# A transformer layer on one core: the first batch's cross tiles move from beside the end of the attention to the middle of it

## The reference

```python
x = x + attn(layernorm(x), wq, wk, wv, wo)      # 32 query heads, 8 key/value heads, head width 64, rope, causal
x = x + xattn(layernorm(x), ctx_2048)           # ctx: (4, 512, 512)
x = x + moe(layernorm(x), Wg, W1, W3, W2, sw1, sw3, sw2)
# xattn: both operands are rounded to fp8 (e4m3) steps in blocks, then out[e,m,n] = sum_k xq[e,m,k] * wq[e,n,k]
#   activations: blocks of 1 token x 128,  scale = max|x| of the block / 448
#   context:     blocks of 128 x 128,      scale = max|w| of the block / 448
# moe: top-1 of 8 experts, 256 places each, hidden width 704, silu(x@W1)*(x@W3) @ W2, plus one shared expert
```

## Time and profile before

| | |
|---|---|
| median of 3 runs | 1580.55 us (1579.67 to 1581.69) |
| the profiled execution's own time | 1581.1 us |
| its span | 1579.3 us |
| PE busy | 1453.4 us (92%) |
| DVE busy | 1205.1 us (76%) |
| POOL busy | 1022.9 us (65%) |
| ACT busy | 959.4 us (61%) |

### The profile page before, as it was taken

How to read it: one execution, slowest core, us unless ns; L and a number is a source line. 1 busy time by engine, 2 the same in 40 slices (tenths; PEclk the granted TensorE clock), 3 DMA queues, 4 the chain that set the end, 5 groups by cost and what they waited for, 6 DMA issues and landing times.

```text
span 1579.3 us, 26942 instructions
## 1 busy us (share of the span) xinstructions
PE 1453.4 (92%) x8617; PEld 1274.5 (81%) x8617; DVE 1205.1 (76%) x2936; ACT 959.4 (61%) x2420; POOL 1022.9 (65%) x1006
## 2 busy tenths in 40 slices
PE   5899999999999999999999997758988887999997
PEld 4788888888878888888888886648888787899996
DVE  7678888887887887887887887976676755577775
ACT  4687777777676787887887886432121213556562
POOL 3787887887777888888898896732121213345555
PEclk9999999999999999999999999888999999899998
DMA  6435534333322433433443432121000003577766
GB/s 205 139 101 165 158 103 128 116 85 109 115 60 59 107 105 90 115 98 95 115 111 86 113 94 67 54 83 60 27 28 28 8 28 124 179 228 223 228 214 237
DMA packets 106812, 177.08 MB, mean 112 GB/s; under 512 B 16886, under 2 KB 38646, under 8 KB 106672
## 3 DMA queue, kind: packets, MB, share of 16 engines
q1 hardware_dynamic: 103920, 166.84, 35.8%
q0 software_dynamic: 2560, 8.25, 1.6%
q10 hardware_dynamic: 192, 0.26, 0.1%
HBM read 97.31 MB, written 31.98 MB: 82 GB/s over the span
## 4 chain that ended last, share of the span: by engine, by line
PE 67%; DVE 15%; ACT 8%; issue 4%; DMA 3%; POOL 2%; SPq 1%; DVEq 0%; ACTq 0%; POOLq 0%
PE bank L429 15%; PE bank L431 14%; PE bank L430 14%; PE bank L481 6%; PE bank L447 4%; PE bank L496 4%; PE bank L497 4%; PE bank L448 4%; ACT P L811 3%; DVE P L1110 2%; PE bank L421 1%; ACT xnx L833 1%; DVE Opair L1145 1%; ACT Otmp L817 1%; DVE work L1059 1%
## 5 line engine op out<-in xcount | busy, mean ns | idle before, releaser
L811 ACT ACTIVATE P<-P,mn 128x512 f32<-128x512 f32 (+3 forms) x512 | 284.8, 557 | 210.5 <-DVE mn L1110 206.6
L1532 POOL TENSOR_TENSOR P<-P,ri 128x128 f32<-128x128 f32 (+3 forms) x512 | 361.4, 737 | 22.4 <-DVE ri L1099 22.3
L1110 DVE CUSTOM_DVE_ANT_0 P<-bank,mask 128x512 f32<-128x512 f32 (+3 forms) x512 | 236.6, 480 | 97.2 <-PE bank L448 95.6
L1151 DVE TENSOR_TENSOR PTl<-bank,PTh 128x512 fp32r<-128x512 f32 (+1 forms) x384 | 229.8, 599 | 33.5 <-ACT PTh L823 30.9
L481 PE MATMUL bank<-ident,P 128*128 128x128 f32 x1280 | 202.6, 273 | 2.5 <-POOL P L1532 2.5
L823 ACT ACTIVATE PTh<-bank 128x512 fp32r<-128x512 f32 (+1 forms) x384 | 197.9, 516 | 6.3 <-PE bank L481 3.2
L447 PE MATMUL bank<-KT,QT 128*128 128x256 f32 (+2 forms) x512 | 188.7, 369 | 10.9 <-DVE mn L1110 10.9
L496 PE MATMUL bank<-PTh,VS 128*128 128x256 f32 (+2 forms) x512 | 163.2, 329 | 13.0 <-DVE PTl L1151 8.9
L429 PE MATMUL bank<-XT,Wh 128*128 128x512 f32 x384 | 162.8, 424 | 9.3 <-DVE XT L1081 3.5
L448 PE MATMUL bank<-KT,QT 128*128 128x256 f32 (+2 forms) x512 | 166.3, 325 | 0.0
L497 PE MATMUL bank<-PTl,VS 128*128 128x256 f32 (+2 forms) x512 | 156.9, 327 | 0.0
(11 more groups left out here) (202 smaller groups left out, 4231.9 us busy)
## 6 DMA issues: line engine op xcount, KB each, us to landing
RW<-in_wf SPq DMA_DIRECT2D x170, 256.0 KB, 3.1
QT<-qh SPq DMA_DIRECT2D x256, 64.0 KB, 2.0
QT<-ql SPq DMA_DIRECT2D x252, 64.0 KB, 2.0
Oraw<-in_wo SPq DMA_DIRECT2D x16, 512.0 KB, 5.3
KT<-KT SPq DMA_DIRECT2D x32, 256.0 KB, 3.0
xnx<-in_ctx SPq DMA_DIRECT2D x32, 256.0 KB, 3.5
Wraw<-in_wqkv SPq DMA_DIRECT2D x9, 768.0 KB, 5.0
saved<-Wh SPq DMA_DIRECT2D x7, 768.0 KB, 3.5
```

Source lines behind the costliest of these rows:

```text
L811: e.activation(pq, pq, ACT.Exp, bias=mn[:, z, qb:qb + 1], scale=-1.0, accum_out=rs[:, z, qb:qb + 1]).then_inc(a_exp, 1)
L1110: e.tensor_tensor_reduce(P[:, z, off[qb]:off[qb] + k], bank[n % 2][:, 0:k], mask[:, 512 - k:512], -0.125, BIG, ALU.add, ALU.min, mn[:, z, ...
L1151: e.tensor_tensor(pt_part(PTl, part), bank[2 + part][:, 0:128 * n].rearrange("p (m n) -> p m n", n=128), pt_part(PTh, part).bitcast(F32), ...
L1532: e.tensor_tensor(pq, pq, ri[:, z, qb:qb + 1].to_broadcast([128, n]), ALU.mult).then_inc(g_norm, 1)
```

## The change

1. `cross_round` of batch 0 (4 tiles) leaves the side slots. Its tiles become four more jobs beside the attention; there are 20 jobs, one every 3 steps from 59 on, in four buffers instead of two. Their statistics are taken on ACT in steps 64 to 72, their inverse roots by DVE and POOL in steps 73 to 76, their block maxima in steps 77 to 82 (ACT norms a tile, DVE reduces it: `look`), and one call makes the scales of all four tiles in step 83 (`first_scales`). ACT norms the tile again when its job comes (`norm_beside`).
2. In a job the DVE parts come one step later than before; `unscaled` comes 6 steps behind `scaled`, so both fall in the same step, every third.
3. The Newton steps of the inverse roots in steps 18, 22 and 26 go to POOL (`newton`).
4. A step from 117 on runs two side slots instead of one, the second at its end. Batch 0's turns, products, norms and expert turns are spread over steps 121 to 130, the context turns of batch 1 go to steps 131 and 132. On DVE the first side slot of a step comes behind `masked(h, 1)` and `join` instead of in front.
5. The statistics behind a `cross_add` become a stage of their own, one slot later (`stats3`).
6. The first weight pieces are loaded in step 126 instead of 128; ACT and POOL split all 11 `Uh` pieces before they wait for the small tables, and the 6 `Dh` pieces inside the first parts of `ffn`.

```diff
@@ def slots():
     first = ("route_turn", "cross_turn", "logits", "choose", "place", "cross_product")
-    for b in range(NB):
+    for i in range(TB):
+        plan(-36 + i, "context_turn", 0, i)
+        plan(-32 + 2 * i, "cross_turn", 0, i)
+        plan(-31 + 2 * i, "cross_product", 0, i)
+        plan(-30 + 2 * i, "stats3", 0, i)
+        plan(-22 + i, "norm3", 0, i)
+        plan(-20 + i, "route_turn", 0, i)
+        plan(-16 + i, "context_turn", 1, i)
+    plan(-23, "rstd3", 0)
+    plan(-4, "logits", 0)
+    plan(-2, "choose", 0)
+    plan(2, "place", 0)
+    for b in range(1, NB):
         s = 16 * (b - 1)
...
@@ def background():
-    return [61 + 4 * j for j in range(NCTX)]
+    return [59 + 3 * j for j in range(NCTX + TB)]
...
+        jobs = [("context", t) for t in range(8)] + [("cross", t) for t in range(TB)]
+        jobs += [("context", t) for t in range(8, NCTX)]
+        YB = [xnx[:, 0, :], xnx[:, 1, :], free_wraw[:, 0:512], free_wraw[:, 512:1024]]
...
@@ scalar_engine
+            def norm_beside(j):
+                t = jobs[j][1]
+                wait_job_buffer(need, j)
+                need.wait_ge(g_root, 25)
+                e.activation(YB[j % 4], X[:, t, :], ACT.Identity, bias=ssum[:, 0, t:t + 1],
+                             scale=rstd[:, t:t + 1]).then_inc(a_norm, 1)
...
-                if h - 6 in begins:
-                    unscaled(begins[h - 6])
+                if h - 7 in begins:
+                    unscaled(begins[h - 7])
                 if h - 1 in begins:
                     scaled(begins[h - 1])
+                if h + 1 in begins and jobs[begins[h + 1]][0] == "cross":
+                    norm_beside(begins[h + 1])
+                if 77 <= h < 81:
+                    look(h - 77)
...
+            for s in (-8, -7, -6):
+                side_slot(s)
+            while len(pieces) > NP - UP:
+                split_piece(0, pieces.pop(0))
             need.wait_ge(d_k, 48)
...
@@ vector_engine
+            def first_scales():
+                need.wait_ge(v_look, TB)
+                scales(aam[:, :, :], asc[:, :, 0, :], asc[:, :, 1, :], 1e-4).then_inc(v_small, 1)
...
-                if h >= NH - 11:
-                    side_slot(h - NH - 15)
                 if 0 <= h < NH:
                     masked(h, 1)
                 if 0 <= h - 3 < NH:
                     join(h - 3)
+                if h >= SIDE:
+                    side_slot(2 * (h - SIDE) - 44)
...
@@ gpsimd_engine
+            def newton(ts, n):
+                v, r, q = mv[:, ts, 1], rstd[:, ts], rtmp[:, ts]
+                need.wait_ge(v_small, 1 + 2 * (n // 3))
+                need.wait_ge(g_root, 4 * n)
+                e.tensor_tensor(q, r, r, ALU.mult).then_inc(g_root, 1)
+                need.wait_ge(g_root, 4 * n + 1)
+                e.tensor_tensor(q, q, v, ALU.mult).then_inc(g_root, 1)
+                need.wait_ge(g_root, 4 * n + 2)
+                e.tensor_scalar(q, q, -0.5, 1.5, ALU.mult, ALU.add).then_inc(g_root, 1)
+                need.wait_ge(g_root, 4 * n + 3)
+                e.tensor_tensor(r, r, q, ALU.mult).then_inc(g_root, 1)
...
@@ sync_engine
                 if h == NH - 8:
                     for t in range(3):
                         load_cw(t)
-                if h == NH:
+                if h == NH - 6:
+                    for t in range(3):
+                        load_t1(t)
+                if h == NH - 2:
                     for _ in range(NR):
                         load_piece()
```

More of the change, by code:

```diff
@@ L1008, in scalar_engine @@
                     ffn(x, k, x == NX - 2)
+                    for _ in range(min(2, len(pieces))):
+                        split_piece(0, pieces.pop(0))
             for s in range(8 * (NX - 1) - 5, max(side) + 1):
@@ L1486, in vector_engine @@
                 side_slot(s)
-                for _ in range(min(4, len(pieces))):
-                    split_piece(0, pieces.pop(0))
+            while len(pieces) > NP - UP:
+                split_piece(0, pieces.pop(0))
             for x in range(NX - 1):
@@ L1784, in load_piece @@
                     need.wait_ge(p_kv, NU)
[L1785 removed]
+                    need.wait_ge(d_keep, 16 * len(jobs))
                 else:
@@ L1803, in side_slot @@
                         load_cw(t + 3)
+                    elif stage == "cross_turn" and t + 3 < TB:
+                        load_t1(t + 3)
                     elif stage == "load_x":
```

272 lines of the change are left out of this document (173 added, 99 removed).

## The result

The changed kernel takes 1562.16 us (median of 4 runs, 1559.33 to 1563.82), the kernel before, on the same chip, 1580.15: ratio 0.9883, 95% interval 0.9866 to 0.9900. Run again later it gave 1560.31, ratio 0.9867 (0.9852 to 0.9883). The forecast was 1554, its range 1542 to 1572. The profiled execution took 1559.33 us, its span is 1557.5. It is the shortest of the four: by the medians the change gives 18.0 us, by the two profiled spans 21.8, and what follows is cut from the latter.

A forecast was written before the change was run, and what follows sets the result against it. PE paces steps 61 to 116; the 118 us from 948.7 to 1066.8 hang on DVE and the boundary's order. Terms -4.1 + 6.5 + 0.2 - 28.3 - 1.1 = -26.8 on 1581.1 gave 1554 by the median, range 1542 to 1572.

The forecast's parts named there:

- Inverse roots: Steps 18 to 30: small DVE instructions move to POOL and lie hidden in its idle time; -4.1 us.
- Twenty jobs: Steps 59 to 124: twenty rounding jobs instead of sixteen beside the attention; +6.5 us, bounds -4 and +16.
- double halves: Steps 72, 84, 96 and 108: both ACT halves of a job delay exponentials, `lower_out` and `join`; 4 x 1.5 = +6.0 us.
- relaxed wait: Rounding jobs: one step more between parts removes DVE's 0.25 us wait for `scaled`; 16 x 0.25 = -4.0 us.
- Steps 121 to 127: End of the attention: with turns and four products these steps take what they took, 63.4 us; +0.2 us.
- Drain: Step 128 to the shared expert's first matmul: less DVE work and a better order, 29.4 us instead of 57.7; -28.3 us.
- Inside the first parts of `ffn`: PE waits 2.4 us for small tables, but context turns leave and clock is regained; -1.1 us, from -4 to +4.
- Later batches: The `stats3` stage and the later batches: no effect, 0.
- C: Rival, slower: ACT's double halves and POOL's backlog make PE wait from step 59 to 118; 1590 us, chance 0.05.
- A: Rival: product steps 123 to 126 don't compress, PE and DVE wait in turn; +14, 1568 us, chance 0.14.
- B: Rival: everything is covered, ACT's double jobs hide and the drain gains more; 1542 us, chance 0.12.
- D: Rival: the boundary only moves, its idle 18.10 us stay at two thirds; 12 less gain, 1566 us, chance 0.09.

The follow-up runs named there:

- e2: Changed kernel with the inverse roots of the last eight tiles back on DVE in steps 22, 25 and 30: 1564.25 us, ratio 0.9895 to the kernel before.
- e5: Changed kernel with the unscaled half, and the keep, of six rounding jobs two steps later: 1557.62 us, ratio 0.9841 to the kernel before.
- e9: Changed kernel with DVE's first side slot of each late step ahead of `masked(h, 1)` again: 1563.59 us, ratio 0.9886 to the kernel before.
- e4: Changed kernel with routing weights in their own buffer, loaded in step 101, rounded right after the attention; triangle copied later: 1557.99 us, ratio 0.9863.
- e8: Changed kernel with the statistics of batches 1 to 3 right behind each product's addition again: 1565.93 us, ratio 0.9900 to the kernel before.
- e10: Changed kernel with DVE's two instructions of each job between `masked(h, 1)` and `join`, not at the step's front: 1585.59 us, ratio 1.0028.

## Why the prediction was right, and where not

- *Inverse roots, -4.1*: measured -4.0, and 3.45 when undone (e2). The price was right; its cause, a DVE instruction that stands while POOL works, was in the earlier trace rows unrecognised. I read "the small DVE instructions" off the one that stood: the earlier trace rows has one of 0.16, shorter than POOL's 0.25, not longer. So the overrun by some 4 us was mine. By the Trainium skill's factor of two (GPSIMD Engine Reference, Key points), an estimate from the 0.17 of an undisturbed one, the four would take POOL 1.4 and fit in its idle 2.16 as well. Measured are 0.20 on POOL against 0.17 on DVE, less than that factor, and the instructions stayed hidden.
- *Twenty jobs, +6.5*: measured **+15.4**, at the upper bound of 16. This is the step that failed. (By its own terms the bound is 14.1, 13.6 + 2.5 + 2.0 - 4.0, so the measured value lies above it.) The double halves were put at four times 1.5; they are six times 1.15 (e5), and the steps behind 102 and 66 were missed. The look was right for step 79 (+2.1), but step 81 pays 1.4 again. The scales cost 1.6, not 2.5. `rstd_first` in step 73 had no term (0.3). The gain of 4 from the relaxed wait is not there, and that is the largest single miss: DVE's wait of 0.25 for `scaled` is gone in all twenty jobs, but it had hardly cost a step anything. Steps 91 and 115 held that wait and a job's first DVE instruction before and hold neither now, and they are only 0.07 and 0.08 shorter (7.48 to 7.41 and 7.40). In their place these instructions stand for POOL, and their sum grew by 8.3 us. The sentence "its products are wanted a step later, so I take nothing" on POOL's extra work left that out: where POOL is at work when such a DVE instruction starts, the rest of POOL's is charged to DVE, whether or not its product is wanted.
- *Steps 121 to 127, +0.2*: -0.6, in part by luck. Steps 121 and 122 took 16.2 for 16.2, and steps 123 to 126 10.6, 9.05, 8.8 and 9.0 for 9.0 each; the load that "may wait 1 us" waited 2.0. Step 127 took 9.0 for 11.2 and covered that. The reason given for choosing PE's work over the bound, the changed place on DVE, was not what kept the product steps near 9: with the old place they take 8.5 (e9).
- *Drain, -28.3*: -30.2. The part up to the last `weigh` took 10.05 for 12.0, the rest 17.5 for 17.4. No PE wait over 2.3 us.
- *Inside the first parts of `ffn`, -1.1*: **+2.9**. The wait of 2.4 for the tables was there (2.70), but behind it the granted clock was 0.65 for 4.9 us. The context turns did leave (PE is busy for 20.8 instead of 22.7), but the wait for the rounding of batch 1's tile grew by as much, 3.94 to 6.09, so they gave nothing. e4 shows 4.8 us in the tables' wait and the clock behind it.
- *Later batches, 0*: -4.7, most of it from the statistics' own slot (e8), which I had put at nothing.

So the sum was -26.8 for -21.8 by the profiled spans, and for -18.0 by the medians. The direction came from the right mechanism, a drain without the roundings and with a better order. That the total came as near as it did is partly luck: two misses of +9 and +4 were more than half covered by a gain of 4.7 that I had not seen, 1.9 more in the drain and 0.8 in steps 121 to 127. The slices of clock 8 in the earlier trace rows begin at 987 us, not at 948; nothing in the sum hangs on it. Of the signs, these failed: step 128 began at 1019, not by 1016; the first `ffn` matmul came at 1046.8, not near 1041; steps 72, 84, 96 and 108 kept their length, and it was the steps behind them that grew, by 1.2 to 2.2; and steps 59 to 118 took 7.66 in the mean, over the 7.6 that was to speak for C. C's double ACT halves and the busy POOL are indeed among what cost 15 us; its price stayed under the 27 from which it decides. A, B and D fell: the product steps compress, the jobs are not covered, and the boundary's idle stretch is gone.

## What to carry to other kernels

Small work beside a loop that PE paces is priced by where it falls in the loop's own period, here four steps: with a job every four PE was idle for only 2.7 of 413.8 us, one every three meets each full step in turn, and at such a meeting 1.15 of an added 1.26 us passed through. Before a wait is priced as a gain, look whether the steps that hold it are longer than those that don't. Before a DVE instruction is placed or made more frequent, look up what GpSimd has under way at that place, and read the spread between its shortest and its longest duration. When an idle boundary is cut, look for the next thing that had been on time only because of it (here the small tables and a queue's order).

## What the runs showed that I had not expected

A DVE instruction with one source of 128x512 takes 0.40 us beside an idle GpSimd and up to 2.22 us beside a busy one, and then ends 0.28 to 0.36 us behind the GpSimd instruction, in 101 of the 102 cases of three profiles (before, after, e10) in which one was under way at its start. It shows no wait in the profile: it is counted as busy. Which of two instructions with starts less than 20 ns apart goes first decides 1.14 us, and so steps in which nothing was changed have two lengths.
